# Attention over slots of four columns, a segment's maximum shared by a backward scan, and no common counter of waits

## The reference, cut to what matters

```python
h = (x @ W.T).reshape(n, H, D)
alpha = a_src . h[src] + a_dst . h[dst] + sum(relu(edge_attr @ edge_W.T + edge_b) * h[dst])   # layer 1
alpha = a_h . h[src] + a_t . h[dst] + a_e . (edge_attr @ W_e)                                # layer 2
alpha = where(alpha >= 0, alpha, 0.2 * alpha)
amax  = segment_max(alpha, dst)
ex    = exp(alpha - amax[dst])
out   = segment_sum(h[src] * ex / segment_sum(ex, dst)[dst], dst) + bias
x     = layernorm(x + out)
```

## Time and profile before

| | us |
|---|---|
| median of 3 runs (8401.17 to 8413.48) | 8402.92 |
| the profiled execution | 8402.59 |
| its span in the trace | 8400.9 |

### The profile page before, as it was taken

One profiled execution on the slowest core, in us unless ns is written; L12 is line 12 of the kernel. 1 busy time (PEld: TensorE's weight loads), 2 busy tenths in 40 slices (PEclk: granted clock), 3 DMA queues, 4 the chain that ended last, 5 costly groups with the idle time before them and its releaser, 6 DMA issues. The chain is left out here.

```text
span 8400.9 us, 99556 instructions
## 1 busy us (share of the span) xinstructions
PE 4341.3 (52%) x18128; PEld 3258.7 (39%) x18128; DVE 5967.1 (71%) x19539; ACT 3318.6 (40%) x8834; POOL 4723.1 (56%) x4730
## 2 busy tenths in 40 slices
PE   8700000999943333377722221001878877899844
PEld 4400000888831111155521111000555555788733
DVE  7756666777778888799967777998444444455577
ACT  5477200788821111178800000444222222344499
POOL 8777677444446666555567776665777777000000
PEclk9855555999965555599955555555888888999955
DMA  9299898777756666599956665887555555566699
GB/s 266 10 301 312 289 300 277 240 243 243 243 172 189 189 188 190 167 325 338 333 168 179 179 179 164 259 259 225 83 84 84 84 84 82 177 202 204 201 353 341
DMA packets 1168036, 1765.41 MB, mean 210 GB/s; under 512 B 255746, under 2 KB 627766, under 8 KB 1167414
## 3 DMA queue, kind: packets, MB, share of 16 engines
q1 hardware_dynamic: 680950, 903.40, 33.1%
q0 software_dynamic: 238720, 537.64, 27.2%
q10 hardware_dynamic: 247744, 318.00, 10.4%
HBM read 968.89 MB, written 840.95 MB: 215 GB/s over the span
## 5 line engine op out<-in xcount | busy, mean ns | idle before, releaser
L662 POOL DMA_INDIRECT st<-S,last_i x1176 | 1113.0, 946 | 970.9 <-DVE yt L703 394.4
L889 POOL DMA_INDIRECT rows<-T,src_i x784 | 740.9, 945 | 251.4 <-issue 237.7
L605 ACT ACTIVATE xo<-z,shift,rsd 128x256 f32<-128x256 f32 x1568 | 853.9, 595 | 4.4 <-issue 4.4
L902 PE MATMUL psE<-encs,attr 4*128 4x256 f32 x784 | 405.2, 668 | 764.8 <-DMA attr<-in_attr3T 762.2
L916 ACT ACTIVATE psX<-diff 128x32 f32<-128x32 f32 x392 | 78.8, 201 | 1651.9 <-DVE diff L964 1651.9
L1099 POOL DMA_INDIRECT A<-comb,ai x392 | 628.8, 1604 | 164.4 <-issue 146.6
L1171 DVE TENSOR_SCALAR eq<-psI,src_f 128x128 f32<-128x128 f32 x392 | 136.7, 349 | 670.9 <-DMA A<-comb,ai 566.0
L902 PE MATMUL psE<-fes,attr 64*128 64x8 f32 x784 | 199.8, 363 | 786.5 <-DMA attr<-in_attr64T 785.0
L902 PEld LDWEIGHTS psE<-encs,attr 4*128 4x128 f32 x784 | 227.3, 319 | 942.4 <-DMA attr<-in_attr3T 901.7
L1113 PE MATMUL psH<-rbf,wf1s 20*128 20x256 f32 x784 | 263.4, 462 | 626.2 <-DMA rbf<-in_rbfT 626.2
L553 PE MATMUL psC<-sums,chain 128*128 128x256 f32 x4 | 2.4, 700 | 1085.5 <-PEq L442 1085.5
(11 more groups left out here) (235 smaller groups left out, 14727.8 us busy)
## 6 DMA issues: line engine op xcount, KB each, us to landing
X<-xo ACTq DMA_DIRECT2D x588, 256.0 KB
xt<-X SPq DMA_DIRECT2D x588, 256.0 KB
S<-sums SPq DMA_DIRECT2D x392, 272.0 KB
S<-sums SPq DMA_DIRECT2D x392, 256.0 KB, 3.9
A<-zero SPq DMA_DIRECT2D x392, 256.0 KB
T<-tt ACTq DMA_DIRECT2D x196, 280.0 KB
T<-tt ACTq DMA_DIRECT2D x196, 272.0 KB
XT<-in_x SPq DMA_DIRECT2D x1, 50176.0 KB
```

Of the source, the lines that this page charges most:

```text
L605: ins = e.activation(y[s][:, k, :], z[s][:, k, :], ACT.Identity, bias=shift[s][:, k, :], scale=rsd[s][:, k, :])
L662: e.indirect_dma_start(st[s][:, k, :], None, sums_table, bass.IndirectOffsetOnAxis(ap=last_i[:, c:c + 1], axis=0))\
L889: e.indirect_dma_start(rows[s][:, k, :], None, table, bass.IndirectOffsetOnAxis(ap=src_i[:, c:c + 1], axis=0))\
L902: mm = e.matmul(psE[s % 2][:, k * EW:(k + 1) * EW], attr[s][:, k, :], weights[:], start=True, stop=True)
```

## The change

- Attention goes in slots of QA = 4 columns over 4 buffers, 98 slots in place of 196, written out by a new helper, written, that takes any number of slots. psE grows to two banks each in layer 1; the rectification becomes two instructions.
- The running maximum of a slot is one forward scan over [head, 5] (the last slot's maximum in front of the four columns) with a penalty table penw; a backward scan with the next column's penalty then gives every column the last running maximum of its segment within the slot. The exponentials take alpha, and the carried maximum, less that one.
- So the factor for the sum so far is needed only at the slot's first column; the other three columns are one multiply-add each, by same (0 or 1), with all operands in SBUF.
- ScalarE copies the maxima to the sums' rows (keep_max), and SyncE's store waits for it too.
- Setup builds penw (3925 columns): a memset and eight copies on VectorE, ahead of what follows there.
- marks is gone everywhere.

```diff
+def written(count, slots, stages):
+    for t in range(count + max(lag for _, lag in stages)):
+        for stage, lag in stages:
+            if 0 <= t - lag < count:
+                stage((t - lag) // slots, (t - lag) % slots)
...
         e.wait_ge(sem, value)
-        if e.engine in alone:
-            e.sem_inc(marks, 1)
...
+        QA = 4
+        penw = sb("penw", [P, (C // QA * H + 1) * (QA + 1)])
...
+                        link(e.memset(penw[:], NONE))
+                        for h in range(H):
+                            by_head = penw[:, 0:C // QA * H * (QA + 1)].rearrange("p (t h g) -> p t h g", h=H, g=QA + 1)
+                            link(e.tensor_copy(by_head[:, :, h, 1:QA + 1], pen[:].rearrange("p (t g) -> p t g", g=QA)))
...
                 hold(e, *done(folded, i, s))
-                e.sem_inc(marks, 1)
...
-                G, NS, LAG = 2, 4, 3
-                R = C // (G * NS)
+                G, NS = QA, 4
+                N = C // G
...
                             hold(e, *done(summed, i, s))
+                            hold(e, *done(maxed, i, s))
                             e.dma_start(nodes(S)[:, c, :], sums[s][:]).then_inc(signal(stored, s), 16)
...
-                            e.activation(psE[s % 2][:], psE[s % 2][:], ACT.Relu).then_inc(signal(rectified, s), 1)
+                            for k in range(0, G, 2):
+                                half = psE[s % 2][:, k * EW:(k + 2) * EW]
+                                ins = e.activation(half, half, ACT.Relu)
+                            ins.then_inc(signal(rectified, s), 1)
...
+                        def keep_max(i, s):
+                            hold(e, *done(scored, i, s))
+                            hold(e, *done(stored, i, s, NS))
+                            e.copy(sums[s][:, :, VW:SW], mb[s][:, :, 1:G + 1].rearrange("p h g -> p g h")).then_inc(signal(maxed, s), 1)
...
-                            for k in range(G):
-                                pc = pen[:, bass.ds(i * (G * NS) + (s * G + k), 1)]
-                                last = sums[s][:, k - 1, VW:SW] if k else sums[(s - 1) % NS][:, G - 1, VW:SW]
-                                e.tensor_scalar(mp[s][:, k, :], last, pc, None, ALU.add)
-                                link(e.scalar_tensor_tensor(sums[s][:, k, VW:SW], last, pc, lg[s][:, k, :], ALU.add, ALU.max))
-                            link(e.tensor_tensor(diff[s][:, :, 0:H], mp[s][:], sums[s][:, :, VW:SW], ALU.subtract))
-                            e.tensor_tensor(diff[s][:, :, H:2 * H], lg[s][:], sums[s][:, :, VW:SW], ALU.subtract).then_inc(signal(scored, s), 1)
+                            e.tensor_tensor(lg[s][:, :, 0], mx[(s - 1) % NS][:, :, G], mx[(s - 1) % NS][:, :, G], ALU.max)
+                            link(e.scalar_tensor_tensor(by_column(lg[s][:, :, 1:G + 1]), dot[s][:], 0.2, dot[s][:], ALU.mult, ALU.max))
...
+                            link(e.tensor_tensor_scan(flat(mx[s][:]), pw, flat(lg[s][:]), 0.0, ALU.add, ALU.max))
+                            link(e.tensor_tensor_scan(flat(mb[s][:])[:, ::-1], nxt[:, ::-1], flat(mx[s][:])[:, ::-1], 0.0, ALU.add, ALU.max))
+                            e.scalar_tensor_tensor(diff[s][:, :, 0], lg[s][:, :, 0], pen[:, bass.ds((i * NS + s) * G, 1)], mb[s][:, :, 1], ALU.add, ALU.subtract)
+                            e.tensor_tensor(diff[s][:, :, 1:G + 1], lg[s][:, :, 1:G + 1], mb[s][:, :, 1:G + 1], ALU.subtract).then_inc(signal(scored, s), 1)
...
+                            e.tensor_tensor(heads(psD[:, 0:VW]), heads(last), r, ALU.mult).then_inc(bsteps, 1)
+                            e.tensor_tensor(v, v, wide(ex[s][:, :, 1:G + 1].rearrange("p h g -> p g h")), ALU.mult).then_inc(bsteps, 1)
+                            e.wait_ge(bsteps, at + 2)
+                            ins = e.tensor_tensor(sums[s][:, 0, 0:VW], psD[:, 0:VW], rows[s][:, 0, 0:VW], ALU.add)
+                            for k in range(1, G):
+                                ins.then_inc(bsteps, 1)
+                                e.wait_ge(bsteps, at + 2 + k)
+                                ins = e.scalar_tensor_tensor(sums[s][:, k, 0:VW], sums[s][:, k - 1, 0:VW], same[:, bass.ds((i * NS + s) * G + k, 1)],
+                                                             rows[s][:, k, 0:VW], ALU.mult, ALU.add)
```

More of the change, by code:

```diff
@@ L62, in total, with total_of @@
     return [(sem, rounds * (16 * dmas if dmas else slots)) for sem in sems]
+def total_of(stage, count):
+    sems, slots, dmas = stage
+    return [(sem, len(range(s, count, slots)) * 16 * dmas) if dmas else (sem, count) for s, sem in enumerate(sems)]
+def written(count, slots, stages):
[3 more added lines that the diff above has]
+                stage((t - lag) // slots, (t - lag) % slots)
 def unrolled(rounds, slots, stages):
[L67 to L70, removed]
+    written(rounds * slots, slots, stages)
 def build(nc, N, x, src, dst, dst_next, ew, rbfT, attr3T, attr64T, w0T, b0, w1T, w1, a1, encW, bias1,
@@ L78, in build @@
     assert C % 8 == 0 and VC % 8 == 0 and 0 < VC < C
-    alone = (nc.sync.engine, nc.gpsimd.engine, nc.scalar.engine)
     used = {}
@@ L840, in attention_edges @@
                 rows, rowsd, sums = tiles("rows", W), tiles("rowsd", WD), tiles("sums", SW)
+                lg, mx, mb, diff = [[ctx.enter_context(sbuf(f"{n}{s}", [P, H, G + 1], F32)) for s in range(NS)] for n in ("lg", "mx", "mb", "diff")]
                 KA = 4 if layer == 1 else attr64T.shape[0]
@@ L922, in _ @@
                         for s in range(NS):
+                            e.memset(mx[s][:], 0.0)
                             ins = e.memset(sums[s][:], 0.0)
@@ L927, in _ @@
                         e.wait_ge(started, 1)
-                        SC = 8 if layer == 1 else 6
+                        SC = 7 if layer == 1 else 5
                         def score(i, s):
@@ L971, in add @@
                             v = rows[s][:, :, 0:VW].rearrange("p g (h w) -> p g h w", h=H)
-                            e.tensor_tensor(v, v, wide(ex[s][:, :, H:2 * H]), ALU.mult)
-                            B = 2 * G - 1
-                            n = 0
-                            for k in range(G):
-                                last = sums[s][:, k - 1, 0:VW] if k else sums[(s - 1) % NS][:, G - 1, 0:VW]
-                                r = ex[s][:, k, 0:H].rearrange("p (h w) -> p h w", w=1).to_broadcast([P, H, HW])
-                                n += 1
-                                e.tensor_tensor(heads(psD[:, 0:VW]), heads(last), r, ALU.mult).then_inc(bsteps, 1)
-                                e.wait_ge(bsteps, i * (NS * B) + (s * B + n))
-                                ins = e.tensor_tensor(sums[s][:, k, 0:VW], psD[:, 0:VW], rows[s][:, k, 0:VW], ALU.add)
-                                if k < G - 1:
-                                    n += 1
-                                    ins.then_inc(bsteps, 1)
-                                    e.wait_ge(bsteps, i * (NS * B) + (s * B + n))
+                            r = ex[s][:, :, 0:1].to_broadcast([P, H, HW])
@@ L986, in add @@
+                            for k in range(1, G):
[3 more added lines that the diff above has]
+                                                             rows[s][:, k, 0:VW], ALU.mult, ALU.add)
                             ins.then_inc(signal(summed, s), 1)
                             hold(e, *done(summed, i, s))
-                        unrolled(R, NS, [(score, 0), (add, 1)])
+                        written(N, NS, [(score, 0), (add, 1)])
@@ L991, in attention_edges @@
                 with nc.Block() as block:
-                    end = sums[NS - 1][:, G - 1, :]
+                    banks.close()
+                    end = sums[(N - 1) % NS][:, G - 1, :]
                     t = lambda n, sh: ctx.enter_context(sbuf(n, sh, F32))
```

46 lines of the change are left out of this document (26 added, 20 removed).

## The result

The changed kernel takes 8165.6 us (median of 4 runs, 8163.2 to 8169.5), the kernel before 8402.1 (8399.6 to 8413.5): ratio 0.9716, 95% interval 0.9703 to 0.9728. It gains 236 us.

A forecast was written before the change was run, and what follows sets the result against it. The prediction took GpSimd's issuing to bound attention 2, and VectorE's work with a chain through SyncE attention 1. 8402.6 - 179.9 + 10 (attention 1) + 13.7 (attention 2) + 7.7 (setup) - 16 (marks) = 8238.1 us, range 8175 to 8300.

The forecast's parts named there:

- the term for the marks: All stages: dropping the semaphore increments saves 16 us, 10 in layer 2 and 6 in the filter, nothing elsewhere.
- Layer 1: Layer 1's node stage: marks cost nothing, hidden by the transfers and by TensorE; without that cover 10 us.
- Layer 2: Layer 2's node stage, VectorE without a pause: a mark costs 0 to 0.11 us, taken as 0.05 x 196 = 10 us.
- The last stages: Filter stage: marks delay scatters, 0.03 x 196 = 6 us saved, 39 at most; marks in other stages after it cost nothing.
- Rival 3: Marks are worth all the rows allow, 39 us in the filter and 22 in layer 2, 61 for 16: 8193 us; 16%.
- Attention 1: Attention 1: four-column slots move the bound from VectorE and the SyncE chain to GpSimd; -179.9 us, then +10 for stretched gathers.
- rival 2: Attention 1 misses GpSimd's floor, attributes late or VectorE's new operations slow; 11 us per slot, 8326 us; 12%.
- Attention 2: Attention 2: GpSimd bounds it before and after; +10 us for stretched gathers and +3.7 for the tail, +13.7.
- The stretch: Both attention stages: multiply-adds with both inputs in SBUF lengthen the gathers, +10 us per stage, bounds 0 and 57.
- Rivals 1: Attention stages: a gather meeting a multiply-add waits until it is over, 29 us per stage, 8276 us; 9%.
- 4: Both attention stages: VectorE stretches every one of 1568 gathers by 0.21 us, 329 us in place of 20, 8547 us; 4%.
- The cover by TensorE: Stages other than layer 2 and filter: transfers and TensorE hide the marks' cost; without cover the same 10 us a stage.

The follow-up runs named there:

- m_no_sync_gpsimd: Kernel before without hold's marks on SyncE and GpSimd, ScalarE's and VectorE's kept, against the kernel before: ratio 1.0004.
- m_no_vector: Kernel before without ln_measure's one mark on VectorE, hold's marks kept, against the kernel before: ratio 0.9972.
- m_no_scalar: Kernel before without hold's marks on ScalarE, those on SyncE, GpSimd and VectorE kept, against the kernel before: ratio 0.9948.
- m_none: Kernel before without any mark, attention as it was: 8659.8 us against 8748.5 for the kernel before, ratio 0.9905.
- a_load: Changed kernel plus 1.3 us more VectorE work (a memset) in every attention slot: 8163.0 us, ratio 0.9726 to the kernel before.
- a_psum: Changed kernel with the sums of columns 1 to 3 in two steps through PSUM: 8152.0 us, ratio 0.9710 to the kernel before.
- a_same: Changed kernel run again, unchanged, on a chip where the kernel before takes 8395.5 us: 8159.1 us, ratio 0.9720.
- b_same: Kernel before run once more, unchanged, with a profile, on the third chip, where a run of the kernel before took 8796.7 us.
- best: Changed kernel with sums through PSUM and penw built at the end of setup: ratio 0.9747 to the kernel before.
- a_marks_et9: Changed kernel with all marks back and layer 1's ET store on SyncE's queue, nine slots behind the loads: ratio 0.9995 to the kernel before.
- best2: Same kernel as best (changed kernel, sums through PSUM, penw built late), run again on the third chip: ratio 0.9757 to the kernel before.

## Why the prediction was wrong

**The step that failed** is the term for the marks: "In the other stages I cost them at nothing, hidden by the transfers and by TensorE; without that cover they would give the same 10 us a stage." It was a term of 16 us and measured 79. Layer 1 alone measured 36, more than three times even the 10 that the sentence gives a stage without cover. Three things were wrong in the term.

- Layer 1 (forecast 0, measured -36). I took the transfers to be its bound, from a DMA share about 1. A hundred us of the middle of that stage, before and then after:

```profile
3800.00:3900.00 100.00, 78.28 (x375) 59.90 (x374) 95.73 (x342) 81.64 (x250) 58.72 (x63) 1.00 1.03 340
```
```profile
3620.00:3720.00 100.00, 82.58 (x396) 63.83 (x396) 99.70 (x363) 83.79 (x262) 61.78 (x66) 1.00 1.05 356
```

  The queues move 356 GB/s as soon as the engines ask for it, so 340 was no limit. VectorE at 96% was the one to see: it ends at 99.7.
- Layer 2 (forecast -10, measured -23). The stage and its mechanism were right. The bounds were 0 to 0.11 per slot, I took 0.05, and it is 0.12: the mark removed the overlap of two short instructions and added a gap. An estimate from half of the gap's bound missed the loss of overlap, which the record of 21 ns doesn't hold either.
- The last stages (forecast -6 for the filter, nothing behind it; measured -3 and -12). ScalarE is at 90% or more in the page's last two slices. Putting all marks back cost 13 us behind the filter (1243.4 against 1230.0) and 8 in it. Behind the filter the four kernels of one chip point to ScalarE's marks: 1249.5 (m_no_sync_gpsimd) and 1253.0 (m_no_vector) with them, 1242.8 (m_no_scalar) and 1241.0 (m_none) without, one profile each.

Rival 3 had the marks at 61 and the time at 8193, and the measured time lies in its band, 8150 to 8205, of which my range cut off 25 us of 55, more than the quarter that I counted. It named the right cause, but that it came so close is in part luck: its 22 for layer 2 were right, its other 39 stood in the filter, where 3 to 8 were, and it left layer 1 out as well.

**What held.**

- Attention 1: 1008.7 forecast, 1005.5 measured: the gathers took 986.2 from first to last (989.3 forecast), the tail 19.4 as forecast, with a score of 4.10 for 4.05 and sums of 3.68 for 3.68. GpSimd's issuing is the bound (a_load), VectorE waits for rows in each slot, and rival 2 is out. VectorE was busy 730 / 98 = 7.5 us per slot, where a step of 7.73 with its small gaps was forecast.
- Attention 2: 1006.2 forecast, 1003.3 measured. Here two errors partly cancel: the gathers stretched by 5.8 in place of 10, and the tail grew by 5.0 in place of 3.7.
- The stretch: +10 per stage forecast, 7 and 6 measured, by the mechanism named (a_psum). Rivals 1 (29 per stage) and 4 (165) are out as averages, though single gathers do reach 1.16 when a multiply-add runs beside them, as in the row above. The Trainium skill, "SBUF — State Buffer", section "Who interferes with whom", says that a VectorE instruction with two inputs in SBUF contends with a GpSimd one that reads SBUF, and that the port pair they share is an exclusive lock. The trace agrees that gathers are held up at times, and its 7 to 15 ns per gather are far from a whole instruction of 494.
- The cover by TensorE, where there is one. In layer 0 TensorE is busy 98% of the stage before the change, and its 13 marks of ScalarE and one of VectorE per slot cost nothing, which fits the cover that the prediction named:

```profile
1472.00:2362.00 890.00, 874.49 (x4704) 750.54 (x4704) 624.25 (x1962) 730.38 (x2156) 371.88 (x392) 0.99 0.76 238
```

- Setup: +7.7 forecast, +6.2 measured; the strided copies go faster than I took them, 3.21 for eight.

## What to carry over

A semaphore increment without work can cost more than its record: on VectorE, where it worked without a pause, one took away the overlap of the instructions at its sides and cost 0.12 us for a record of 0.021. Before calling such marks free, count them per slot on every engine of a stage in which some compute engine has next to no idle time; in layer 1 VectorE was 96% busy, and ScalarE's marks cost the stage 30 us though ScalarE itself was busy 82%. A DMA share of 1 is no proof of a bound on transfers; ask which engine has no idle time first.

When a group waits for another and both are close, make the slower one faster only down to the next bound: here 5 us per four gathers was GpSimd's floor, and all that VectorE gains beyond it is worth nothing. And ask whether the bound is the same on another chip, as the next section shows.

## What the runs showed that I had not expected

- The same kernel before took about 8400 us in the first result and beside a_same, and 8748, 8793 and 8812 on three other chips. Hop 0 takes 520 to 523 us in the former and 584 to 600 on the others, attention 2 992 to 1005 and 1144 to 1220 for changed and unchanged kernels together, while layer 0 (890 to 901), layer 2 and the filter barely move. It lies in the stages of gathers, but for attention 1 of the kernel before, which takes 1179 us on the first chip and 1182 in b_same. In best's attention 1 the gathers' length is the same 948 ns, but they wait for sums again:

```profile
L901 POOL DMA_INDIRECT rowsd<-T,dst_i x174 | 165.0, 948 | 118.7 <-DVE sums L1010 63.9 <-issue 48.4 <-DMA xt<-in_x 6.4
```

  What makes those chips slower is open. It takes away most of the change's gain: a_marks_et9, with all marks and slots of four columns, has 1184 and 1210 us in the two attention stages where b_same on that chip has 1182 and 1216, and its ratio is 0.9995 (0.9983 to 1.0007). The 173 us of attention 1 are a result of the first kind of chip. On the slower ones the marks still count, and the version with the sums through PSUM gains 2.5% (best2: 1150 and 1145 in attention); the changed kernel itself ran on none of them.
- The marks of SyncE and GpSimd, almost 6000 of them (3669 and 2309), cost nothing in the time as a whole, 1.0004 (0.9994 to 1.0013), though single stages moved by up to 50 us either way without them. In the changed kernel, on the chip of a_same, where GpSimd's issuing bounds both attention stages, these take the same time with all marks and without, within 2 us.
